# A channel norm whose variance is averaged from squares in two fp32r parts

## The reference

```
def _ln_c(v, eps=1e-06):
    m = jnp.mean(v, axis=1, keepdims=True)
    s = jnp.var(v, axis=1, keepdims=True)
    return (v - m) / jnp.sqrt(s + eps)

x = x + _L0_conv_ref(_ln_c(x), L0_conv_w_l, L0_conv_b_l, L0_conv_w_r, L0_conv_b_r)
```

## Time and profile before

| | us |
|---|---|
| median of 3 runs | 2552.9 (2551.2 to 2553.08) |
| the profiled execution | 2551.47 |
| its span, first to last instruction | 2549.6 |
| the first stage in it, first load to last add | about 0 to 196 |
| TensorE busy in the span | 1811.4 (71%) |
| VectorE busy | 1460.1 (57%) |
| ScalarE busy | 1144.1 (45%) |
| GpSimd busy | 1100.1 (43%) |

### The profile page before, as it was taken

The page is one execution under the profiler, slowest core; times in us unless marked ns, Lnnn a source line. Parts: engine busy times, 40 slices in busy tenths (PEclk is TensorE's granted clock), DMA queues, the critical chain, the costliest instruction groups (busy, mean ns, idle before and its releaser), DMA issues. The chain is left out here.

```text
span 2549.6 us, 32816 instructions
## 1 busy us (share of the span) xinstructions
PE 1811.4 (71%) x8144; PEld 1045.0 (41%) x8144; DVE 1460.1 (57%) x3427; ACT 1144.1 (45%) x2248; POOL 1100.1 (43%) x1400
## 2 busy tenths in 40 slices
PE   8986433332424318999999997488888883798887
PEld 4652221221212105555555553265565552343333
DVE  6651466666565625666666664276666664345445
ACT  5650111111111106777677774254544552566665
POOL 3330046766666673333333333777777740000000
PEclk9997655555555558999999998599999996899999
DMA  5457521221222001111111111133333322755551
GB/s 171 157 139 161 146 66 57 68 61 52 71 59 74 27 25 47 58 56 57 56 58 57 56 58 51 25 102 102 102 102 111 104 92 90 180 159 166 152 173 62
DMA packets 189502, 230.31 MB, mean 90 GB/s; under 512 B 56531, under 2 KB 170804, under 8 KB 189236
## 3 DMA queue, kind: packets, MB, share of 16 engines
q1 hardware_dynamic: 164276, 202.60, 27.0%
q0 software_dynamic: 25088, 26.14, 4.3%
HBM read 111.73 MB, written 116.88 MB: 90 GB/s over the span
## 5 line engine op out<-in xcount | busy, mean ns | idle before, releaser
L646 POOL DMA_INDIRECT scr_rows<-row,place_int x392 | 404.9, 1033 | 124.3 <-issue 124.3
L1243 POOL DMA_INDIRECT y_returned<-scr_y,place_of_token x392 | 377.1, 962 | 132.4 <-issue 116.8
L673 PE MATMUL token_psum<-centre_and_gate,x_now 128*128 128x144 f32 x392 | 102.2, 452 | 346.9 <-DVE x_now L802 346.9
L1025 POOL CAST w_now<-w1all 128x512 fp32r x252 | 155.0, 615 | 376.3 <-PE y_psum L1061 364.2
L1108 ACT ACTIVATE hidden<-hidden_psum,w_now 128x512 f32<-128x512 f32 x504 | 304.5, 691 | 1.2 <-PE hidden_psum L1050 1.2
L1050 PE MATMUL hidden_psum<-page_tokens,w_now 128*128 128x512 f32 x1008 | 268.9, 409 | 1.6 <-DVE page_tokens L1136 1.6
L1061 PE MATMUL y_psum<-hidden,w_now 128*64 128x512 f32 x1008 | 244.1, 605 | 0.0
L673 PEld LDWEIGHTS token_psum<-centre_and_gate,x_now 128*128 128x128 f32 x392 | 93.9, 331 | 365.9 <-issue 334.0
L1050 PEld LDWEIGHTS hidden_psum<-page_tokens,w_now 128*128 128x128 f32 x1008 | 180.4, 189 | 136.6 <-issue 100.6
L203 PE MATMUL ln_var<-ln_sq,average 128*128 128x448 f32 x448 | 210.2, 554 | 22.4 <-DVE ln_q L225 20.0
L225 DVE SCALAR_TENSOR_TENSOR ln_q<-ln_var,ln_rr 128x448 f32<-128x448 f32 x224 | 138.9, 620 | 151.9 <-ACT ln_rr L220 151.5
(11 more groups left out here) (204 smaller groups left out, 3417.7 us busy)
## 6 DMA issues: line engine op xcount, KB each, us to landing
tokens<-scr_split SPq DMA_DIRECT2D x112, 224.0 KB, 3.7
page_rows<-scr_rows SPq DMA_DIRECT2D x126, 132.0 KB, 2.1
scr_y<-y_rows SPq DMA_DIRECT2D x126, 128.0 KB, 1.7
scr_rows<-zero_rows SPq DMA_DIRECT2D x14, 924.0 KB, 4.3
scr_xn<-xn SPq DMA_DIRECT2D x56, 224.0 KB, 2.0
scr_split<-hi SPq DMA_DIRECT2D x56, 224.0 KB, 2.5
scr_split<-lo SPq DMA_DIRECT2D x56, 224.0 KB, 2.7
tokens_plus_y<-scr_xn SPq DMA_DIRECT2D x56, 224.0 KB, 2.7
```

The lines of the kernel that those rows point to most:

```text
L646: pool.indirect_dma_start(out=R, out_offset=bass.IndirectOffsetOnAxis(ap=idx[:, u, 2 * px + a:2 * px + a + 1], axis=0), in_=row[:, u, px, ...
L673: mm = pe.matmul(tps[:, b, q, (P + 2 * E) * s:(P + 2 * E) * (s + 1)], xa[:, b, PG * k:PG * k + PG], cenw[:], start=True, stop=True)
L1025: pool.tensor_copy(w1s[:, b, t].rearrange("p l h -> p (l h)"), w1all[:, bass.ds(e, 1)].rearrange("p o l h -> p (o l h)")).then_inc(w_done, 1)
L1243: pool.indirect_dma_start(out=y[:, h % 3, k // 2, k % 2, :], out_offset=None, in_=Y, in_offset=bass.IndirectOffsetOnAxis(ap=PLACE[:, at:at ...
```

## The change

The norm of the first stage is built with `split`. ScalarE squares the centred tile twice, once into an fp32r buffer `sq_hi` and once into the fp32 buffer `sq`. GpSimd subtracts the first from the second and writes the rest as fp32r into `sq_lo`. TensorE averages both with fp32r products that accumulate in the same PSUM buffer, with `avgr`, a copy of `AVG` in fp32r that ScalarE makes once. GpSimd's step is now: lo of n, then the add of n-1, with one step more at the end. One semaphore for constants is shared by all stages instead of one for each, so the later waits for it count from an offset.

```diff
+    consts = sem(top, "constants")
+    BEFORE3, BEFORE5, BEFORE6, BEFORE7 = 48, 160, 208, 256
...
-            ln = Norm(ctx, "ln1", 4, 2)
+            avgr = sbuf(ctx, "average_r", [P, P], F32R)
+            ln = Norm(ctx, "ln1", 4, 2, split=avgr)
+            avg_cast = sem(ctx, "p1_avg_cast")
...
                     pe.wait_ge(consts, 48)
+                    pe.wait_ge(avg_cast, 1)
...
                 def _(act):
+                    act.wait_ge(consts, 48)
+                    act.activation(avgr[:], AVG[:], ACT.Copy).then_inc(avg_cast, 1)
                     act.wait_ge(eps_set, 2)
...
                     def step(n, m):
-                        pool.wait_ge(ln.normed, n + 1)
-                        x = tile(X, n)
-                        pool.tensor_tensor(x, x, xn[:, m % 4], ALU.add).then_inc(added, 1)
+                        if exists(n):
+                            ln.pool_square_lo(pool, n, m)
+                        if exists(n - 1):
+                            pool.wait_ge(ln.normed, n)
+                            x = tile(X, n - 1)
+                            pool.tensor_tensor(x, x, xn[:, (m - 1) % 4], ALU.add).then_inc(added, 1)
                         if isinstance(n, int) and n == UNIT - 1:
                             pool.wait_ge(w1_hi, 1)
                             pool.tensor_tensor(w1all[:, :, 1, :], w1raw[:], w1all[:, :, 0, :].bitcast(F32), ALU.subtract).then_inc(w1_lo, 1)
 
-                    every_tile(pool, step, UNIT, 0)
+                    every_tile(pool, step, UNIT, 1)
...
-                    sp.wait_ge(consts, 16 * 7)
+                    sp.wait_ge(consts, BEFORE3 + 16 * 7)
```

More of the change, by code:

```diff
@@ L272, in build @@
             gps = psum(ctx, "gate_psum", [P, 2, 512])
-            ln = Norm(ctx, "ln1", 4, 2)
+            avgr = sbuf(ctx, "average_r", [P, P], F32R)
+            ln = Norm(ctx, "ln1", 4, 2, split=avgr)
+            avg_cast = sem(ctx, "p1_avg_cast")
             w1raw = sbuf(ctx, "w1raw", [P, E, H0])
             w1_in, w1_hi, w1_lo = (sem(ctx, "p1_" + s) for s in ("w1_in", "w1_hi", "w1_lo"))
-            consts, eps_set, x_in, added = (sem(ctx, "p1_" + s) for s in ("consts", "eps", "x", "added"))
+            eps_set, x_in, added = (sem(ctx, "p1_" + s) for s in ("eps", "x", "added"))
             part_ready, part_copied = sem(ctx, "p1_part"), sem(ctx, "p1_part_copied")
@@ L563, in build @@
                                               "squared", "summed", "kept"))
-            consts, zeroed, seeded, routed, totalled, ranked, dummy, named_done = (
-                sem(ctx, "p3_" + s) for s in ("consts", "zeroed", "seeded", "routed", "totalled", "ranked", "dummy",
+            zeroed, seeded, routed, totalled, ranked, dummy, named_done = (
+                sem(ctx, "p3_" + s) for s in ("zeroed", "seeded", "routed", "totalled", "ranked", "dummy",
                                               "named"))
@@ L658, in _ @@
                 def _(pe):
-                    pe.wait_ge(consts, 16 * 6)
+                    pe.wait_ge(consts, BEFORE3 + 16 * 6)
                     pe.matmul(vps[:, 0, 0:2 * E], CEN[:], wg[:], start=True, stop=True).then_inc(folded, 1)
@@ L782, in _ @@
                     dve.memset(NL[:], 0.0).then_inc(prepared, 1)
-                    dve.wait_ge(consts, 16 * 6)
+                    dve.wait_ge(consts, BEFORE3 + 16 * 6)
                     dve.tensor_copy(before[:], raw[:]).then_inc(prepared, 1)
@@ L1196, in build @@
             ln4 = Norm(ctx, "ln4", 2, 1, depth=1)
-            consts, signed, zeroed, pad_hi_done, pad_lo_done, conv_done, x3_done, hi_done, lo_done = (
-                sem(ctx, "p5_" + s) for s in ("consts", "signed", "zeroed", "pad_hi", "pad_lo", "conv", "x3", "hi", "lo"))
+            signed, zeroed, pad_hi_done, pad_lo_done, conv_done, x3_done, hi_done, lo_done = (
+                sem(ctx, "p5_" + s) for s in ("signed", "zeroed", "pad_hi", "pad_lo", "conv", "x3", "hi", "lo"))
             moved, x2_done = sem(ctx, "p5_moved"), sem(ctx, "p5_x2")
@@ L1325, in _ @@
                             high3(n)
-                    act.wait_ge(consts, 48)
+                    act.wait_ge(consts, BEFORE5 + 48)
                     act.activation(cw[:], cwraw[:], ACT.Sign).then_inc(signed, 1)
@@ L1379, in _ @@
                         low3(n)
-                    dve.wait_ge(consts, 48)
+                    dve.wait_ge(consts, BEFORE5 + 48)
                     for n in range(NT + 2):
@@ L1418, in build @@
             w1_in, w1_hi, w1_lo = (sem(ctx, "p6_" + s) for s in ("w1_in", "w1_hi", "w1_lo"))
-            consts, s_v, s_mm, s_a, s_out = (sem(ctx, "p6_" + s) for s in ("consts", "v", "mm", "a", "out"))
+            s_v, s_mm, s_a, s_out = (sem(ctx, "p6_" + s) for s in ("v", "mm", "a", "out"))
             steps, marks = [0], {}
@@ L1440, in shifted_exp @@
                         link(dve.tensor_tensor(dst[:], t3["ex"][:], bc(ri[:]), ALU.mult))
-                    dve.wait_ge(consts, 48)
+                    dve.wait_ge(consts, BEFORE6 + 48)
                     link(dve.memset(ones[:], 1.0))
@@ L1490, in _ @@
                 def _(pe):
-                    pe.wait_ge(consts, 48)
+                    pe.wait_ge(consts, BEFORE6 + 48)
                     pe.wait_ge(s_v, marks["mean"])
@@ L1551, in build @@
             ln = Norm(ctx, "ln5", 4, 2, group=KT, xc=xc)
-            consts, idx_in, w2_done, b2_a, b2_done, up_done, gelu_done, down_done, u_done, scaled, out_done = (
-                sem(ctx, "p7_" + s) for s in ("consts", "idx", "w2", "b2a", "b2", "up", "gelu", "down", "u",
+            idx_in, w2_done, b2_a, b2_done, up_done, gelu_done, down_done, u_done, scaled, out_done = (
+                sem(ctx, "p7_" + s) for s in ("idx", "w2", "b2a", "b2", "up", "gelu", "down", "u",
                                               "scaled", "out"))
@@ L1710, in _ @@
                 def _(dve):
-                    dve.wait_ge(consts, 7 * 16)
+                    dve.wait_ge(consts, BEFORE7 + 7 * 16)
                     def weigh(p, b):
```

## The result

The changed kernel takes 2593.5 us (median of 4 runs, 2588.4 to 2595.1), the kernel before on the same chip 2552.1 (4 runs, 2548.6 to 2553.1). The ratio is 1.0161, with a 95% interval of 1.0144 to 1.0179: slower by 41 us.

A forecast was written before the change was run, and what follows sets the result against it. TensorE was taken to bound the first stage at 3.05 us per tile. 47 x 3.65 = 171.6, + 4.5 = 176.1 against 143.3, with the end +35.6: 2588, 8-in-10 range 2568 to 2602.

The forecast's parts named there:

- The order on GpSimd: GpSimd queue, first stage: lo(n+2) stands behind add(n), which waits for xn(n); pace goes from 3.05 to 3.65 us.
- the whole round of 6.51: First stage, from lo(n) through xn(n) and add(n) to lo(n+2) without blocking: 6.51 us for two tiles, 3.26 per tile.
- The blocked g: VectorE's g(n), requested 3.85 us after lo(n) starts, waits for GpSimd's lo(n+1) and ends 0.48 after it.
- the 3.65: Pace per tile with g blocked: lo(n+1) 1.14, g's end 0.48, xn 0.13, add 0.80, lo(n+2) 1.10 us.
- The second rival: First stage: g issues just ahead of lo(n+1), which waits; 3.34 us per tile, 2573, or 2569 without blocking; 14%.
- TensorE keeps the pace: Rival, first stage: the TensorE saving reaches the path, 2.62 us per tile, 20 us less, 2533; 7%.
- The w1 subtraction: GpSimd's 4.51 us expert-weight subtraction now stands between add(6) and lo(8): 4.5 us once, 3.6 if g(7) precedes lo(8).
- The copy of the averaging matrix: ScalarE's copy delays the first centring product, but the load of tiles 1 to 7 hides it: nothing, some 2 us uncovered.
- The stores at nothing: xn(n) waits for the store of tile n-4; 0 taken, 10 us being the other end.
- The end of the stage: After xn(47): part 47's copy comes 1.4 us later and xn(55) 1.4 more after xn(52), together 2.8.
- The clock, a rival at 5%: First stage: TensorE may fall to its lower clock level, 3.9 to 5.2 us per tile, 2600 to 2660; 5%.
- TensorE's 2.62: TensorE's work per tile in us with the fp32r variance pair costing 0.41 instead of the old product's 0.84.

The follow-up runs named there:

- g unblocked: The changed kernel with r written to a PSUM bank, the variance keeping one bank instead of two: 2584.7 us, ratio 1.0119.
- single loads: x loaded one tile after each store instead of in eights: on the changed kernel 2590.9 us, on the add two behind 2548.0, on the kernel before 2550.6.
- three repairs: Changed kernel with the add two tiles behind, tile-by-tile loads of x, and stores of tiles 48 to 51 between the gate-row loads: 2538.6 us, ratio 0.9954.

## Why the prediction was right, and where its sizes were off

2588 was forecast, 2593.5 measured, inside the range and on the slower side. Point by point:

**The order on GpSimd: shown.** Moving the add by one more tile takes the loss away; moving it the other way multiplies it by five (+202 us for +41), and at full clock a tile there takes 6.47 to 6.49, the whole round of 6.51 as summed; taking TensorE out of the ring also removes the loss. TensorE's own cost is no cause, since the pair is cheaper than the old product.

**The blocked g: shown in size.** Each link of the 3.65 stands in the timeline within 0.03. With g unblocked the pace is 3.27, against 3.26 summed. The second rival, g first (3.34 per tile), happens only now and then: nine of the 56 low parts take 1.50 to 1.55, with single loads three (tiles near the start, behind the subtraction and behind tile 52). So it is mostly a disturbance that brings it about, and the loop returns to the blocked form by itself.

**TensorE keeps the pace: refuted** for this order, and right (2.70 for 2.62) once the order and the loads allow it.

**The w1 subtraction: right up to tile 8, and short by 1.0 behind it.** Tiles 0 to 8 were forecast at 33.7, measured 33.65. That the six gaps before it add up to the ring's 21.9 is partly luck, since they run from 2.34 to 4.70. The next low part is late and waits for g besides:

```profile
41.53 4.50 POOL L426 TENSOR_TENSOR w1all<-w1raw,w1all 128x2048 fp32r<-128x2048 f32 x1
45.99 1.50 POOL L191 TENSOR_TENSOR ln_sq_lo<-ln_sq,ln_sq_hi 128x448 fp32r<-128x448 f32 x1
```

**The copy of the averaging matrix at nothing: right.** xn(0) starts 0.1 later than before.

**The stores at nothing: mis-sized, by about 2.3 us.** Tiles 8 to 47 took 3.5 more than the 142.4 summed. Of these, 1.0 is the gap from tile 8 to 9, which is 4.65, and 2.5 lie behind tile 9. With single loads only 0.2 are left behind tile 9, so 2.3 are the stores'.

**The clock behind the subtraction: left out, 1.0 us.** The gap from tile 8 to 9 stays with single loads (5.05), and the rows show where it comes from. TensorE stands for 5.42 us until the low part behind the subtraction is made, and then runs at the lower of its two levels, with a granted clock of 0.50 until 51.05. The gate products from 48.67 to 51.05 take 2.38 instead of 1.35. The low part of the next tile is finished at 49.70, but its variance pair starts only at 52.01, behind them and a centring, with TensorE never idle in between:

```profile
47.63 0.74 PE L200 MATMUL ln_var<-ln_sq_hi,average_r 128*128 128x448 f32 x1 [5.42 <-POOL ln_sq_lo L191]
...
52.01 0.71 PE L200 MATMUL ln_var<-ln_sq_hi,average_r 128*128 128x448 f32 x1
```
```profile
47.63:51.05 3.42, 3.42 (x26) 2.52 (x26) 0.97 (x2) 1.36 (x3) 2.07 (x2) 0.50 0.14 36
```

In the kernel before the subtraction makes no such pause: the clock is 1.00 from 40 to 60 us. No run has this pause at full clock, so the 1.0 is read from the rows and not from an experiment.

**The end of the stage: mis-sized, by 1.3 in all.** Up to xn(52) +1.1 was measured for +1.4. Behind it +3.1 for +1.4, and here too the clock matters, which the step had left out. TensorE has stood for 9.54 us, and the rows are VectorE's, GpSimd's, TensorE's and ScalarE's, then the stretch 228 to 236:

```profile
224.10 0.62 DVE L237 SCALAR_TENSOR_TENSOR xn<-ln_xc,ln_g 128x448 f32<-128x448 f32 x1 [8.62 <-DMA scr_xlr<-xn]
...
225.29 1.23 DVE L230 SCALAR_TENSOR_TENSOR ln_g<-ln_q,ln_r 128x448 f32<-128x448 f32 x1
...
225.99 1.51 POOL L191 TENSOR_TENSOR ln_sq_lo<-ln_sq,ln_sq_hi 128x448 fp32r<-128x448 f32 x1
...
227.56 0.74 PE L200 MATMUL ln_var<-ln_sq_hi,average_r 128*128 128x448 f32 x1 [9.54 <-POOL ln_sq_lo L191]
228.10 0.57 PE L201 MATMUL ln_var<-ln_sq_lo,average_r 128*128 128x448 f32 x1
...
228.71 0.63 ACT L216 ACTIVATE ln_r<-ln_var,eps 128x448 f32<-128x448 f32 x1 [9.68 <-PE ln_var L201]
```
```profile
228.00:236.00 8.00, 7.56 (x85) 5.76 (x87) 3.75 (x6) 3.25 (x8) 3.29 (x4) 0.69 0.27 72
```

The pair's products are 0.54 apart instead of 0.30, r follows the second by 0.61 instead of 0.40, and the low part is held up by g for 0.38: together 0.8, which is how late xn(54) is. The other 0.9 comes in the next tile: its low part is finished at 229.69, but its variance pair starts only at 230.99, behind the gate products that began at 228.61 and take 2.38 instead of 1.35. The 1.3 of the end and the 3.5 of tiles 8 to 47 make 4.8 of the 5.5 us between forecast and median.

**The clock, a rival at 5%: didn't happen as a general fall.** It is 0.95 over the middle, with the pace that the ring gives. But the forecast had named a clock under 0.95 before 160 us as a sign of being wrong, and that sign stood in two stretches, 0.91 from 20 to 40 us and 0.83 from 40 to 60. Its argument, that TensorE stands for 1 us at a time, missed the two long pauses, 5.42 and 9.54 us.

**TensorE's 2.62: mis-sized**, 2.70, which changed nothing at 3.65 but caps what the split can bring: 47 x 0.35 = 16 us here, not 20.

**Where the expected gain goes.** In the changed kernel it is idle time of TensorE. With the add two behind, the pace has it (2.71) and the stores take it back (mean 3.08). With single loads the middle keeps most of it, and the end of the stage takes back part. It takes three repairs before a product that is 0.35 us cheaper shows in the total.

## What to carry to other kernels

Before giving an engine new work, write out its queue and ask what its old work waits for: new work early in a chain, queued behind old work from the chain's end, closes a ring over tiles, and the ring's length divided by the tiles in it is the new pace if it is longer than what the engines need, however idle each engine is. The cure here was to put the old work one more tile behind, and it cost no buffer. And a product that gets cheaper uncovers what it had been hiding, here stores behind large loads on one queue, so look at those waits before counting the gain.

## What was not expected of the hardware

Blocking between VectorE and GpSimd goes both ways. Before, only g was seen to wait. In the changed kernel a low part that starts while g runs takes 1.50 or 1.51 instead of 1.13, and GpSimd's add takes 1.36 in the version with the low part on VectorE. In the versions where TensorE doesn't wait for the low part, its mean is 1.50 and 1.43. The Trainium skill (SBUF — State Buffer, Who interferes with whom) says that the order of issue decides who blocks, so GpSimd must block too when VectorE's instruction with two SBUF inputs comes first. No row of before could show that half, and the trace agrees with it. What the blocked one still takes after the other's end is a little less than its full time: 0.48 or 0.49 of 0.62 for g, and 0.98 of 1.13 for the low part (behind the g's that end at 46.51 and 226.52).

TensorE's clock was lower in stretches of the changed kernel (0.91 from 20 to 40 us and 0.83 from 40 to 60, then 1.00 from 60 to 120) though its work per tile had become less. In the version with the add first it went from one level to the other between neighbouring tiles, 0.50 and then 1.00, with pauses of 1.63 and 1.62 us before the variance products of both.
